# Turning softmax probabilities on VectorE instead of TensorE in a windowed-attention layer, with the weighting as four 32-row groups

## The reference

```python
def attn_layer(x, Wqkv, qs, ksc, Wo):            # 16 heads of 64, windows of 32 tokens
    q, k, v = heads(x @ Wqkv)
    q, k = rotary(l2norm(q) * qs), rotary_inv(l2norm(k) * ksc)
    # each window of 32 queries sees its own 32 keys and the 32 before them
    sim = einsum('bhwie,bhwje->bhwij', bq, look(bk)) * 8.0
    attn = softmax(where(mask, -max, sim), -1)    # [32 queries, 64 keys] per window and head
    out = einsum('bhwij,bhwje->bhwie', attn, look(bv))
    return out.reshape(b, n, 1024) @ Wo
for i in range(6):
    x = attn_layer(shift_tokens(x), ...) + x
    x = ffn_layer(shift_tokens(x), ...) + x
```

## Time and profile before

| | |
|---|---|
| median of 3 runs | 3252.57 us (3249.82 to 3264.21) |
| the profiled execution, its own time | 3251.62 us |
| its span | 3249.6 us |
| TensorE, TensorE weight load | 2461.4 us, 1470.9 us |
| VectorE, ScalarE, GpSimd | 2272.3 us, 1733.3 us, 1583.7 us |
| mean granted TensorE clock | 0.906 of full speed |

### The profile page before, as it was taken

The page is one execution under the profiler, slowest core; times in us unless marked ns, Lnnn a source line. Parts: engine busy times, 40 slices in busy tenths (PEclk is TensorE's granted clock), DMA queues, the critical chain, the costliest instruction groups (busy, mean ns, idle before and its releaser), DMA issues.

```text
span 3249.6 us, 47514 instructions
## 1 busy us (share of the span) xinstructions
PE 2461.4 (76%) x17700; PEld 1470.9 (45%) x17844; DVE 2272.3 (70%) x1982; ACT 1733.3 (53%) x1827; POOL 1583.7 (49%) x1678
## 2 busy tenths in 40 slices
PE   2767674888898889888988898889888365767253
PEld 1212122655665666666656666666555112211153
DVE  2765447998888888888888888888885275545301
ACT  1534453666666666666766676667664132544100
POOL 0000005877777777777777777777773000000202
PEclk7988897999999999999999999999999578889677
DMA  4001100000000000000000000000000100110122
GB/s 146 20 27 38 42 1 1 14 1 14 1 1 22 5 10 1 23 1 14 1 22 1 14 1 23 1 14 1 8 1 1 37 23 24 42 50 5 29 68 65
DMA packets 59823, 66.44 MB, mean 20 GB/s; under 512 B 12551, under 2 KB 50309, under 8 KB 57797
## 3 DMA queue, kind: packets, MB, share of 16 engines
q1 hardware_dynamic: 57460, 58.63, 6.2%
q0 software_dynamic: 2128, 4.72, 0.6%
HBM read 46.04 MB, written 17.56 MB: 20 GB/s over the span
## 4 chain that ended last, share of the span: by engine, by line
PE 32%; DVE 18%; issue 17%; POOL 15%; ACT 11%; DMA 5%; SPq 1%; POOLq 1%; ACTq 0%; DVEq 0%; PEldq 0%
DVE big L1276 6%; PE bank L712 5%; POOL small L503 4%; DMA pxs<-part_rows 4%; PE bank L793 4%; ACT big L1047 3%; PE bank L754 3%; DVE big L1354 3%; PE bank L785 2%; POOL small L504 2%; PE bank L836 2%; ACT big L1076 2%; PE bank L830 2%; POOL big L514 2%; DVE small L1332 2%
## 5 line engine op out<-in xcount | busy, mean ns | idle before, releaser
L519 POOL TENSOR_TENSOR sc<-sc,small 128x1024 f32<-128x1024 f32 x96 | 263.5, 2744 | 331.5 <-DVE small L1375 331.5
L1354 DVE TENSOR_TENSOR big<-big,small 128x1024 f32<-128x1024 f32 x192 | 377.5, 1966 | 35.1 <-POOL small L506 35.1
L1276 DVE TENSOR_REDUCE big<-bank 128x2 f32<-128x1024 f32 x256 | 292.7, 1213 | 135.3 <-PE bank L626 135.3
L793 PE MATMUL bank<-pxs,mw 128*128 128x256 f32 x1536 | 369.7, 384 | 0.0
L712 PE MATMUL bank<-wqk,xs 128*128 128x512 f32 x768 | 347.3, 595 | 22.0 <-ACT xs L1063 22.0
L626 PE MATMUL bank<-pxs 128*128 128x512 bf16 x496 | 162.2, 426 | 237.6 <-DMA pxs<-part_rows 146.7
L793 PEld LDWEIGHTS bank<-pxs,mw 128*128 128x128 f32 x1536 | 293.5, 194 | 100.5 <-issue 68.7
L1332 DVE TENSOR_REDUCE small<-big 128x32 f32<-128x2048 f32 x96 | 219.3, 2284 | 127.4 <-ACT big L1076 120.3
L554 POOL DMA_INDIRECT dispatch_rows<-sc,qks x16 | 15.6, 972 | 504.8 <-DVE qks L1523 500.2
L503 POOL TENSOR_TENSOR small<-small 128x32 f32<-128x32 f32 x288 | 244.9, 850 | 32.6 <-DVE small L1334 17.6
L1091 ACT ACTIVATE sc<-bank 128x1024 f32<-128x1024 f32 x96 | 98.3, 1024 | 303.5 <-PE bank L763 303.5
(11 more groups left out here) (206 smaller groups left out, 5033.9 us busy)
## 6 DMA issues: line engine op xcount, KB each, us to landing
pxs<-part_rows SPq DMA_DIRECT2D x32, 448.0 KB
part_rows<-big SPq DMA_DIRECT2D x96, 128.0 KB
wqk<-in_L_ffn_w SPq DMA_DIRECT2D x32, 256.0 KB, 3.0
wqk<-in_L_ffn_Wqkv SPq DMA_DIRECT2D x12, 512.0 KB, 4.4
wvt<-in_wv_layers_t SPq DMA_DIRECT2D x6, 512.0 KB, 5.1
wol<-in_L_ffn_Wo SPq DMA_DIRECT2D x6, 512.0 KB, 5.8
w<-in_L_ffn_W SPq DMA_DIRECT2D x6, 341.0 KB
dispatch_rows<-pxs SPq DMA_DIRECT2D x5, 256.0 KB, 6.5
```

The source lines that it names most:

```text
L519: pool.tensor_tensor(p3, p3, rden(i).unsqueeze(2).broadcast_to([P, LH, 64]), ALU.mult).then_inc(l_pn, 1)
L793: m = pe.matmul(bank[:, 6, part * 2 * P:(part + 1) * 2 * P], mw[:, c, r, :], pxs[:, part, c, r, :], start=(c == 0 and r == 0), stop=(c == ...
L1276: dve.tensor_reduce(nm[:, qt, 2 * p:2 * p + 2], bank[:, 2 * (u % 3):2 * (u % 3) + 2, :], AX.X, ALU.max, negate=True).then_inc(a_mx, 1)
L1354: dve.tensor_tensor(r3, r3, nrm(i)[:, half * LH:(half + 1) * LH].unsqueeze(2).broadcast_to([P, LH, LD]), ALU.mult).then_inc((l_yq, l_yk)[h ...
```

## The change

Three things change, all in the layer slots.

1. The probabilities are no longer turned by TensorE and evicted by ScalarE. One VectorE instruction over 128x1024 elements turns every 32x32 block in place of its own (`turn_probs` is now VectorE's). Window w's 32 queries lie on partitions 32w to 32w+31. After the turn these partitions hold half of the keys of window w, and the other half stands 32 columns further.
2. `turn_windows` makes two plain transposes of X, one shifted by 32 tokens (`xnat`), in place of the four doubled windows. ScalarE evicts 256 columns instead of 512.
3. `weigh` makes eight matmuls of 32 rows x 512 columns in four row groups, two per window that add up in PSUM, and each window has a bank of its own. Both halves of its result are signalled in its second pass.

```diff
@@ TensorE
                 if half == 1 and not (isinstance(T, int) and T < 2):
-                        pe.wait_ge(l_pe, T - 2)
+                    pe.wait_ge(l_kd, 2 * T - 2)
...
-            def turn_probs(T, i):
-                pe.wait_ge(l_pn, T + 1)
-                for c in range(PAIRS):
-                    t = pe.transpose(bank[:, c // 4, (c % 4) * P:(c % 4 + 1) * P], probs(i)[:, c * P:(c + 1) * P], ident[:, :])
-                t.then_inc(l_pt, 1)
...
-                for w in range(4):
-                    s = i * P + w * WIN
-                    for r in range(2):
-                        m = pe.matmul(bank[64 * r:64 * r + 64, 4, w * P:(w + 1) * P], xs[:, b % 2, s:s + 2 * WIN], ident[:, :],
-                                      start=True, stop=True)
-                m.then_inc(l_xt, 1)
+                for half in range(2):
+                    s = i * P + half * WIN
+                    t = pe.transpose(bank[:, 4, half * P:(half + 1) * P], xs[:, b % 2, s:s + P], ident[:, :])
+                t.then_inc(l_xt, 1)
...
+            def weigh(T, i):
+
+                p4 = sc[:, 2, :].rearrange("p (h v t) -> p h v t", h=LH, v=2)
+                for half in range(2):
+                    for w in range(4):
+                        m = pe.matmul(bank[:, (4, 5, 2, 3)[w], :], xnat[32 * w:32 * w + 32, i % 2, half, :],
+                                      p4[32 * w:32 * w + 32, :, half, :], start=(half == 0), stop=(half == 1),
+                                      tile_position=(32 * w, 0), skip_group_check=True)
+                        if half == 1 and w % 2 == 1:
+                            m.then_inc(l_px, 1)
...
                 if not (first and i == 0):
-                    pe.wait_ge(l_pe, T)
+                    pe.wait_ge(l_pt, T)
                     pe.wait_ge(l_e, T + 1)
-                    weigh(T - 1, i + 3, 0)
                     if ahead >= 2:
                         pe.wait_ge(l_raw, 2 * T + 5)
...
-                    weigh(T - 1, i + 3, 1)
+                    weigh(T - 1, i + 3)
@@ ScalarE
-            def turned_probs(T):
-                act.wait_ge(l_pt, T + 1)
-                act.activation(sc[:, 2, :], bank[:, 0:2, :].rearrange("p a t -> p (a t)"), ACT.Copy).then_inc(l_pe, 1)
...
-                if not (first and i == 0):
-                    turned_probs(T - 1)
                 exponentials(T, i)
@@ VectorE
+            def turn_probs(T, i):
+                if not (isinstance(T, int) and T == 0):
+                    dve.wait_ge(l_px, 2 * T)
+                dve.wait_ge(l_pn, T + 1)
+                settle(dve)
+                dve.transpose(sc[:, 2, :], probs(i)).then_inc(l_pt, 1)
...
                 if ahead >= 1:
                     square_sums(T + 1, (i + 1) % 2)
+                if not (first and i == 0):
+                    turn_probs(T - 1, (i - 1) % 2)
+                if ahead >= 1:
                     turn_plain(T + 1, (i + 1) % TILES)
```

More of the change, by code:

```diff
@@ L142, in build @@
         pxs = sb("pxs", [P, 2, PAIRS, 2, 2 * P])
-        xnw = sb("xnw", [P, 2, 4, P])
+        xnat = sb("xnat", [P, 2, 2, P])
         pflat = pxs[:, :, :, :, :].rearrange("p a c r t -> p (a c r t)")
@@ L241, in build @@
         l_tk, l_tq, l_kd, l_qe, l_kh = (sem(n) for n in ("l_tk", "l_tq", "l_kd", "l_qe", "l_kh"))
-        l_s, l_mx, l_e, l_p, l_dn, l_rd, l_pn, l_pt, l_pe = (
-            sem(n) for n in ("l_s", "l_mx", "l_e", "l_p", "l_dn", "l_rd", "l_pn", "l_pt", "l_pe"))
+        l_s, l_mx, l_e, l_p, l_dn, l_rd, l_pn, l_pt = (
+            sem(n) for n in ("l_s", "l_mx", "l_e", "l_p", "l_dn", "l_rd", "l_pn", "l_pt"))
         l_xt, l_xe, l_px, l_pc, l_mm, l_mw, l_m, l_res, l_xf, l_fn = (
@@ L770, in turn_windows @@
                     pe.wait_ge(l_pc, 2 * T - 1)
-                for w in range(4):
-                    s = i * P + w * WIN
-                    for r in range(2):
-                        m = pe.matmul(bank[64 * r:64 * r + 64, 4, w * P:(w + 1) * P], xs[:, b % 2, s:s + 2 * WIN], ident[:, :],
-                                      start=True, stop=True)
-                m.then_inc(l_xt, 1)
-            def weigh(T, i, half):
-                for w in range(2 * half, 2 * half + 2):
-                    for r in range(2):
-                        o = (4, 2)[half] + r
-                        dst = bank[:, o, :].rearrange("p (c v t) -> p c v t", c=PAIRS, v=2)[:, :, w % 2, :]
-                        src = sc[64 * r:64 * r + 64, 2, :].rearrange("p (c t) -> p c t", t=P)[:, :, w * WIN:(w + 1) * WIN]
-                        m = pe.matmul(dst, xnw[64 * r:64 * r + 64, i % 2, w, :], src, start=True, stop=True,
-                                      tile_position=(64 * r, 0), skip_group_check=True)
-                m.then_inc(l_px, 1)
+                for half in range(2):
[11 more added lines that the diff above has]
+                            m.then_inc(l_px, 1)
             def mix(l, b, part, j):
@@ L925, in _ @@
             pe.wait_ge(l_xe, N)
-            turn_probs(N - 1, 3)
-            pe.wait_ge(l_pe, N)
-            weigh(N - 1, 3, 0)
+            pe.wait_ge(l_pt, N)
             pe.wait_ge(l_pc, 2 * N - 2)
-            weigh(N - 1, 3, 1)
+            settle(pe)
+            weigh(N - 1, 3)
             for i in range(3):
```

14 lines of the change are left out of this document (5 added, 9 removed).

## The result

The changed kernel takes 3268.35 us (median of 20 runs, 3255.82 to 3283.25), the kernel before 3249.48 (median of 20, 3237.18 to 3264.21). The ratio is 1.0054, with a 95% interval of 1.0041 to 1.0066: slower by some 18 us. The profiled execution took 3255.82 us itself, with a span of 3253.8, and happens to be the fastest of the 20. So I compare stretches of the trace, and not the spans.

What follows compares the result with a forecast made beforehand. The prediction took a GpSimd-VectorE loop to bound slots 1 to 3, and VectorE's own work slot 0. 16 + 13 - 1 = +28 on 3251.6 gives 3279.6, and so 3280 us, range 3246 to 3325.

Steps and rivals of the forecast that it cites:

- the case of the forecast: Whole kernel: the forecast's own outcome, 3268 to 3295 us, chance 0.40; the turn at 0.75 us gives 3268.
- two large terms: Turn's uncovered cost in slot 0, +16 us, and GpSimd's longer inverse root in slots 1 to 3, +13 us.
- The bound: Slots 1 to 3: GpSimd and VectorE form a loop without spare time, 19.53 us a slot; L1354 absorbs the turn, cost 0.
- The price of the turn: VectorE's turn takes 1.25 us and, with one input in SBUF, excludes no GpSimd operation.
- TensorE's relief at nothing: TensorE gains 1.7 us a slot, 160 us in all, put at nothing because the loop doesn't pass through it.
- Slot 0, +16: Slot 0: turn costs 24 x 1.25 = 30 us; 16 covered by score waits, less 2 for single waits; sum +16.
- The root, +13: GpSimd's inverse root meets all of L1339 and L1344: +0.23 in 47 slots, 11 us, and +0.1 in 24, 2 us.
- just in time: Before `weigh`: the exponential 1.25 later brings `take` to 1323.1 us, and `weigh` wants to start at 1323.4.
- The weighting: TensorE's `weigh`: four row groups overlap, 1.72 us taken, costing the same as before; 2.24 by the skill's factor.
- The clock: TensorE: idle more, so if its granted clock drops more often, scores come late and times rise; no size given.
- The rival of two cycles an element: VectorE's turn runs slower: +1.1 x 24 in slot 0 and about 8 where `take` is late, 3316 us; chance 0.12.
- next to nothing: Rival: slot 0 is better covered and GpSimd's root keeps its 6.62 us, about 3262 us; chance 0.18.

Runs made afterwards that it cites:

- The turn behind the products: Changed kernel with VectorE's turn moved behind L1317 and L1322, the product with the rotation table and the sum: ratio 1.0052, 3269.23 us.
- The second turn: Changed kernel with the turn done twice at its place, the first into a tile that nothing reads: ratio 1.0195, 3319.30 us.

## Why the prediction was right, and where its sum was off

The forecast was 3280 us in a range of 3246 to 3325, with 64% for slower. It came to 3268, slower, and the case of the forecast (3268 to 3295 by itself) just holds it. The mechanism was right: a turn that is covered in three slots of four and paid for in slot 0, and a relief of TensorE that brings nothing. Its two large terms came to 8.8 for 16 in slot 0, and to 10.8 for 13 in the other slots. That the second is so near is partly luck. It adds up -3.2, +9.1 and +4.9, and the root, for which the 13 stood, is only a part of these. Point by point:

- **The bound.** Right for slots 1 to 3. The turn there is absorbed by L1332, which shrank from 3.36 to 2.71 and still ended 1.08 behind L514. Slot 1 stayed at 12.22 from L1312 to the reciprocal.
- **The price of the turn.** 1.237 us on average in 96 (forecast 1.25), and it excludes nothing: 226 small operations of GpSimd lie wholly inside a turn, and take 0.23 to 0.28.
- **TensorE's relief at nothing.** Right in the net, as the kernel without the turn shows (0.9995). In slot 0 the forecast counted on "TensorE's scores now come earlier". That holds only in part. In 13 of the 23 slots 0 TensorE waits for ScalarE's queries, as it did before in 14. Timeline of ScalarE in the changed kernel around one of these:

```profile
1430.76 1.92 ACT L1061 ACTIVATE big<-big 128x2048 f32<-128x2048 f32 x1
1432.56 0.39 ACT L1090 ACTIVATE xnat<-bank 128x256 f32<-128x256 f32 x1
1432.96 1.28 ACT L1102 ACT_TABLE_LOAD   x1
1434.26 0.69 ACT L1102 ACTIVATE hT<-bank,eps 128x512 f32<-128x512 f32 x1
1434.84 2.05 ACT L1067 ACTIVATE kD<-bank 64x1024 f32<-64x1024 f32 x2
1436.91 1.02 ACT L1072 ACTIVATE qT<-bank 128x1024 f32<-128x1024 f32 x1
```

And of TensorE:

```profile
1438.18 1.95 PE L751 MATMUL bank<-kD,qT 128*32 128x128 f32 x64 [2.91 <-ACT qT L1072]
...
1447.24 2.00 PE L772 MATMUL bank<-sc,xnat 32*128 32x512 f32 x16 [1.75 <-ACT big L1053]
```

  ScalarE works without a gap from the squares to the queries, and TensorE waits 2.91 for them, about as long as before (3.05 in this slot). VectorE waited at most 0.5 us there before. Its longer waits (1.0 to 2.0) were in slots 0 of sequences 2 and 3 in which TensorE doesn't wait for the queries, and works in part at half clock ahead of the scores. There the scores do come earlier: in tiles 20, 24, 36 and 40 they ended 5.71, 5.49, 5.70 and 4.83 us after the slot's start, and now 3.43, 3.96, 3.41 and 3.73. In slots 1 the scores stand behind a feed-forward part that waits for ScalarE's gates, 53.0 us in all before and 22.4 now.
- **Slot 0, +16.** It came to +8.8. Of its parts the turn is 28.2 us (forecast 30), and the waits for the scores took 12.9 of them (forecast 14). The other 6 or 7 I had not counted: VectorE's products there are shorter than before, L1322 by 2.6 over the 24 slots, L1317 by 1.1 and L1338 by 1.3, and 1.2 of the wait behind L1338 and 0.9 of that before L1332 are gone. Added to the kernel before, the turn cost +14.7 in slot 0. Most of these 5.9 more are the 5.1 us for which VectorE still waits for the scores there and not here. The forecast also counted 24 turns, and there are 23: the first slot has none.
- **The root, +13.** Right in kind, half in size. Its mean rose by 0.13 in slot 2 (forecast 0.23), by 0.20 in slot 3, and in slot 1 by 0.01 (forecast 0.1): 23 x 0.13 + 23 x 0.20 = 7.6. The forecast compared a made-up sum, 6.85, with the row of one slot. In the trace, L506 and L503 together take 3.46, not 3.54, and the 0.15 for which the product was to wait first isn't there: L1317 starts right behind the turn. The turn behind the products took 6.6 out of slots 2 and 3, which is what one expects if this growth reaches the time. But the root isn't all of it. In slot 3 its mean is already 6.74 without the turn (6.59 before, 6.79 after). And with the turn behind the products slot 2 has a shorter root than before (6.48 against 6.69), and its sum is still 6.8 above before.
- **Not in the sum.** In the five slots 2 in which VectorE also builds the rotation tables it took 12.20 from L1334 to the reciprocal, and now 13.07 in three and 12.36 in two: with that much more work the turn is no longer wholly covered. The three are those in which the clock was at half ahead of the slot. And from the reciprocal to the next L1312 slot 2 grew by 3.5: the squares are late. That isn't `take`, for which the weighting waits in two slots 2 only. From tile 10 on, TensorE was at half clock just ahead of the slot in 10 of the 21 slots 2 of the changed kernel, and in none of the kernel before. A slot of sequence 2 lasts 0.34 longer for it, and one of sequence 4 0.31; ten times that is some 3 of slot 2's 9.1 us (an estimate). In slot 1 it goes the other way. Three slots of the kernel before had the scores at half clock and lasted 0.9 longer than the rest, and none of the changed kernel has, which is most of slot 1's -3.2. I had called `take` just in time. Over the stage the weighting waited 43 us for it, 32 of them in slots 0 and 3, and only the first half of the old weighting was free to go ahead of it.
- **The weighting.** 2.00 us, four row groups at a time, as taken from four column groups. The Trainium skill's factor of 3.07 ("TensorE: Matmul & The Clock Gate", Measured speedup vs the span model) would make it 2.24. The trace doesn't agree: groups of four start 0.43 apart, one instruction's time.
- **The clock.** It fell from 0.98 to 0.96 in the stage, and to 0.94 without the turn. The forecast named this in its last sentence and put no price on it. It has one, as the table of single slots shows. Eight instructions of L782 took 1.89 us at 1.00 and 3.62 at 0.50, and VectorE then waited for the scores.
- **Sums.** Two are slightly off in the forecast, with no effect on it. The rival of two cycles an element comes to 3314 and not 3316, and the chance of "slower" adds up to 0.66 before anything of "next to nothing" is added, not 0.64.

## What to carry to other kernels

Take work from an engine only after asking what its next instruction waits for. Here TensorE lost 105 us of work and no time was won. In over half of the slots 0 its scores wait for ScalarE, and where they don't, stretches at half clock, which became more frequent, took back what was saved. So compare the granted clock before and after, slot by slot, before calling a relief worthless. Work that is added to an engine has a price by its place: this turn costs 18 us at the start of a slot and nothing measurable at the end, where the small operation behind it is held anyway. And a cover must be measured on every chain behind the added work. The second turn ended the cover in slot 2 through TensorE's feed-forward part and the squares behind it, while the loop with GpSimd still had something left.

## What the runs showed of the hardware

- An operation of VectorE with one small input can be held as long as a product. L1311, 128x32, took 0.18 us in the 10 slots where GpSimd was idle at its start. In the other 86 it ended 0.036 to 0.063 us after the operation that GpSimd was then at, 85 times a swap and once the copy, and took up to 2.25. The reduces and the turn beside it were never held. The Trainium skill, "SBUF — State Buffer", Who interferes with whom, counts this kind of operation among those that can take the shared ports although they have one input; the trace agrees.
- Matmuls of different row groups don't wait for the order of issue: two groups issued behind six more instructions of the first two started 0.03 us after them. The Trainium skill, "TensorE: Matmul & The Clock Gate", The mechanism, says that weights for a free row group are pulled ahead of matmuls in flight, and the trace agrees. It also says that the matmuls themselves start and end strictly in order, and there the trace doesn't agree: the last instruction of the first pair, which signals its end, started at 1322.360, 1.37 us after the second pair had begun.
- TensorE's granted clock has a price where its work lies ahead of a wait: eight instructions over 128x256 took 1.89 us at 1.00 and 3.62 at 0.50 (1.2 GHz). VectorE then waited 2.40 us for the scores behind them.
- The turn of 128x1024 f32 in blocks of 32x32 takes as long as a copy-like operation of that size, 1.23 to 1.25 us.
